# A three-stage transformer kernel on one NeuronCore: first-stage waits and row statistics moved, the first expert block's weights in halves

## The chip, the cores and the metric

The kernel runs on one core of a Trainium2 chip. A core has TensorE (matmuls, PE in the rows, its weight loads PEld), VectorE (DVE), ScalarE (ACT), GpSimd (POOL) and SyncE (SP), which here only issues transfers. Each engine runs its own queue in order, and engines wait for one another by semaphores: `wait_ge(s, n)` holds the queue until s has reached n. The metric is the device time of the whole program in microseconds (us), the median of several runs.

## The reference

Four layers follow one another on x of 8 x 512 tokens of 256 numbers, each added to x with a gate:

```python
x = x + tanh(g_xattn[0]) * L0_xattn(layernorm(x), ctx, ctx)   # attention among the 16 heads of one token
x = x + tanh(g_ffn[0])   * L0_ffn(layernorm(x))               # 256 -> 1024 -> 256, quantised to 8 bits
x = x + tanh(g_xattn[1]) * L1_xattn(ctx, layernorm(x), mask)  # masked cross attention, 512 x 512 per head
x = x + tanh(g_ffn[1])   * L1_ffn(layernorm(x))               # 8 experts, 2 for each token
# L0 attention: score = einsum('bsid,bsjd->bsij', Q, K) / 4, softmax over j, times V
# an expert: (silu(x @ w1) * (x @ w3)) @ w2, weighted by the token's share
```

## The kernel before

x lies in SBUF as `X`, 32 tiles of 128 tokens. Three functions run in turn, with a barrier between them.

`first_layer` computes the first two layers in rounds t = -3 to 38; in one round different tiles are at different steps. For tile t: statistics of its rows, `normalise`, transposes and three projections on TensorE (`qkv`), copies of them on ScalarE (`kv_copy`, `q_copy`), products of queries and keys split between VectorE (`own_scores`) and GpSimd (`scores`), the sum of the products on TensorE (`add_scores`), `largest` on VectorE, `exp` on ScalarE, products with the values on VectorE (`own_values`) and GpSimd (`weighted`, line 296), their sums on VectorE (`other_values`, line 602), and the output projection. The feed-forward part of a pair of tiles runs some rounds behind; its row statistics are taken by ScalarE (`f_statistics`, lines 426 to 432), and GpSimd turns them into deviations (`f_deviations`, lines 273 and 275). The order in each engine's queue is that of the calls in its loop over the rounds.

The statistics ahead of `normalise` are made differently: VectorE takes them for whole parts of X (`x_stats`, line 666: tiles 0 to 3, 4 to 15, 16 to 31) and GpSimd makes the deviations of a part at once (`x_deviations`, line 266). The parts are three loads (`x_part`). VectorE also splits the biases of the projections into three bfloat16 rows (`split_biases`), and ScalarE sends these to three partitions (`bias3`, line 418). TensorE starts its rounds when the four weights and `bias3` are in (`w_in` at 5 x 16). ScalarE copies the feed-forward weights at the end of round -1 (`f_weights`, lines 508 to 511), and VectorE makes `w1_lo` from it (line 647).

`cross_attention` is the second stage; of it only two counters of constants change. At its end tokens are scattered to their experts' rows in `expert_in`.

`experts` works through 39 blocks of 256 or 128 rows (`slot`), all of one expert each. Every weight is split in a high and a low part, and a product takes three matmuls. For block j: SP loads w1, w3, w2 of its expert into `raw` (one buffer for each of the three; `load_weights`, line 1758; the next block may load when the low part is made, `lo_done`), ScalarE makes the high part (`high_part`, line 1764), VectorE the low part (`low_part`, line 1768). TensorE computes `hidden`: for f = 0 to 7 the products with w1 and w3 (12 matmuls, line 1918), ScalarE silu (line 1989), VectorE the product `gated` (line 2033); part f of 4 and over waits for `gated` f - 3. Then TensorE transposes the next block's rows (`turn`, line 1911) and does `project` with w2 in four pairs of f, each after its low part (`g_parts`). In block j ScalarE makes the high parts of block j + 1 after silu 1, 3 and 5, and VectorE the low parts after gates 1 and 5 and after the gates. The first two blocks' expert is known early; the expert and first row of the others come from a chain of small one-partition operations of VectorE (lines 2068 to 2107, the last releases `blocks_known`), four of them wide (from line 2092, 592 elements). After that VectorE makes block 0's low parts. Ahead of block 0 TensorE waits for the first high part and runs 16 matmuls of the identity (line 1953).

## Time and profile before

| | us |
|---|---|
| median of 3 runs (2059.53 to 2062.3) | 2061.55 |
| the profiled execution's own time | 2063.94 |
| its span, first to last instruction | 2062.2 |
| busy: TensorE / VectorE / ScalarE / GpSimd | 1892.7 / 1552.3 / 1145.8 / 935.7 |
| first stage, second stage, experts (about) | 0 to 514, to 1375, to 2062 |

The numbers of an instruction come from one execution, so they are compared with its own time. A time in brackets behind an instruction is how long its engine sat idle ahead of it, and the arrow names what ended that.

### The profile page before, as it was taken

Reading aid. Unit: us, or ns where it says so; the run is one execution under the profiler, and the core shown is the slowest. Engines: PE = TensorE matmul, PEld = TensorE weight load, DVE = VectorE, ACT = ScalarE, POOL = GpSimd, SP = SyncE. Lnnn points to the kernel's source line nnn. Section 1 sums busy time; section 2 is a strip of 40 time slices with the busy share of each in tenths; the row PEclk is TensorE's granted clock in tenths of the full one; section 3 lists DMA queues with packets and bytes.
Section 4 is the critical chain, followed back from the end, with each engine's and each line's share of the span. In section 5 each row is a group of like instructions: output and inputs, shape, how many; then the busy total and the mean of one; then the engine's idle time right before and its main releaser. Section 6 shows DMA issues by size and latency. Waiting matters only on the chain. (4 is left out here: it accounts for less than half of the span.)

```text
span 2062.2 us, 35515 instructions
## 1 busy us (share of the span) xinstructions
PE 1892.7 (92%) x12100; PEld 1339.9 (65%) x12100; DVE 1552.3 (75%) x3251; ACT 1145.8 (56%) x2414; POOL 935.7 (45%) x674
## 2 busy tenths in 40 slices
PE   4899999986889999998999999959999999999998
PEld 2566776664543434443434343449999999999998
DVE  7999999992566677777767678657777777777785
ACT  2356666655336555555555555516665665656563
POOL 6999999981633334343534351023222231222322
PEclk9999999997999999999999999979999999999999
DMA  5222222210425051524242423037666666666662
GB/s 176 114 93 114 91 113 114 108 37 1 116 65 124 27 129 53 123 68 108 68 110 73 104 92 77 19 108 251 238 224 234 229 230 209 226 226 231 231 226 89
DMA packets 138569, 271.45 MB, mean 132 GB/s; under 512 B 13244, under 2 KB 90256, under 8 KB 132499
## 3 DMA queue, kind: packets, MB, share of 16 engines
q1 hardware_dynamic: 127916, 243.63, 37.9%
q0 software_dynamic: 9952, 25.25, 3.3%
q8 instruction: 99, 1.62, 0.3%
q14 instruction: 84, 0.68, 0.1%
q10 hardware_dynamic: 518, 0.27, 0.0%
HBM read 200.12 MB, written 70.47 MB: 131 GB/s over the span
## 5 line engine op out<-in xcount | busy, mean ns | idle before, releaser
L1476 DVE CUSTOM_DVE_ANT_0 x_dump<-x_ps,x_bias_q 128x512 bf16<-128x512 f32 x512 | 353.1, 690 | 103.0 <-PE x_ps L1160 90.1
L1345 ACT ACTIVATE x_PT<-x_ps 128x512 f32<-128x512 f32 x512 | 292.2, 601 | 230.6 <-PE x_ps L1175 227.4
L1989 ACT ACTIVATE X<-m_ps 128x256 f32<-128x256 f32 (+1 forms) x312 | 113.1, 363 | 222.0 <-PE m_ps L1918 219.6
L1160 PE MATMUL x_ps<-x_KS,x_QS 96*128 96x512 bf16 x512 | 198.1, 387 | 23.1 <-DVE x_mx L1476 22.2
L1872 POOL DMA_INDIRECT out_dram<-e_y,e_label x71 | 71.6, 1008 | 321.6 <-DVE e_y L2051 302.2
L1174 PE MATMUL x_ps<-x_bias_k,x_ident_b 128*128 128x512 bf16 x512 | 196.6, 384 | 2.8 <-DMA x_QS<-x_rows 1.7
L1175 PE MATMUL x_ps<-x_QS,x_KS 98*128 98x512 bf16 x512 | 196.5, 384 | 0.0
L1918 PE MATMUL m_ps<-e_x_lo,m_hi 128*128 128x256 f32 (+1 forms) x640 | 180.1, 281 | 4.5 <-issue 4.5
L1918 PE MATMUL m_ps<-e_x_hi,m_hi 128*128 128x256 f32 (+1 forms) x640 | 180.0, 281 | 0.0
L1918 PE MATMUL m_ps<-e_x_hi,m_lo 128*128 128x256 f32 (+1 forms) x640 | 179.9, 281 | 0.0
L2033 DVE TENSOR_TENSOR X<-X,m_ps 128x256 f32<-128x256 f32 (+1 forms) x312 | 114.0, 394 | 83.8 <-ACT X L1989 80.0
L1864 POOL DMA_INDIRECT e_y<-out_dram,e_label x71 | 101.8, 1434 | 164.8 <-DMA out_dram<-e_y,e_label 83.2
L296 POOL TENSOR_TENSOR a_pool_pv<-a_e,a_v 128x2304 f32<-128x2304 f32 x32 | 162.8, 5087 | 16.0 <-ACT a_e L478 16.0
L1918 PE MATMUL m_ps<-e_x_hi,e_hi 128*128 128x256 f32 (+1 forms) x608 | 169.8, 279 | 0.0
L1918 PE MATMUL m_ps<-e_x_hi,e_lo 128*128 128x256 f32 (+1 forms) x608 | 169.5, 279 | 0.0
L1918 PE MATMUL m_ps<-e_x_lo,e_hi 128*128 128x256 f32 (+1 forms) x608 | 169.5, 279 | 0.0
L1768 DVE TENSOR_TENSOR m_lo<-m_raw,m_hi 128x2048 fp32r<-128x2048 f32 x60 | 137.3, 2288 | 28.8 <-ACT m_hi L1764 28.8
L1768 DVE TENSOR_TENSOR e_lo<-m_raw,e_hi 128x2048 fp32r<-128x2048 f32 x57 | 130.4, 2287 | 26.8 <-ACT e_hi L1764 26.8
L1160 PEld LDWEIGHTS x_ps<-x_KS,x_QS 96*128 96x128 bf16 x512 | 50.1, 98 | 135.5 <-DVE x_mx L1476 104.9
L1918 PEld LDWEIGHTS m_ps<-e_x_lo,m_hi 128*128 128x128 f32 x640 | 121.8, 190 | 4.6 <-issue 4.6
L1918 PEld LDWEIGHTS m_ps<-e_x_hi,m_lo 128*128 128x128 f32 x640 | 121.8, 190 | 0.0
L1918 PEld LDWEIGHTS m_ps<-e_x_hi,m_hi 128*128 128x128 f32 x640 | 121.7, 190 | 0.0
(344 smaller groups left out, 5413.5 us busy)
## 6 DMA issues: line engine op xcount, KB each, us to landing
m_raw<-in_L_ffn_w_dram SPq DMA_DIRECT2D x117, 1024.0 KB, 5.1
expert_in<-a_blank SPq DMA_DIRECT2D x34, 1032.0 KB, 4.4
parts<-x_part SPq DMA_DIRECT2D x24, 512.0 KB, 3.8
m_x<-expert_in SPq DMA_DIRECT2D x32, 258.0 KB, 4.9
next_mask_k<-in_maskT_dram SPq DMA_DIRECT2D x32, 256.0 KB, 2.6
next_mask_q<-in_mask_dram SPq DMA_DIRECT2D x29, 256.0 KB, 2.8
x_KS<-parts SPq DMA_DIRECT2D x16, 384.0 KB, 11.3
x_QS<-parts SPq DMA_DIRECT2D x8, 576.0 KB, 6.7
```

Source lines behind the costliest of these rows:

```text
L296: pool.tensor_tensor(heads(pool_pv[:, :], PV_POOL), probabilities(e_[t % 2][:, PV_OWN * H:], PV_POOL), values(v_sb[t % 3][:, :], PV_POOL), ...
L1160: pe.matmul(ps_max[m % 2], QS[b % 2][0:HROWS, h, q * P:(q + 1) * P], KS[b % 2][0:HROWS, h, :], start=True, stop=True).then_inc(s1_ps, 1)
L1174: pe.matmul(ps_st[e % 3], ident_b[:, :], bias_k[b % 2][:, kc, :], start=True, stop=False)
L1175: pe.matmul(ps_st[e % 3], KS[b % 2][:, h, kc * P:(kc + 1) * P], QS[b % 2][0:HROWS + MROWS, h, :], start=False, stop=True).then_inc(st_read ...
L1345: act.activation(PT[unit % 2][:, k, :], ps_st[e % 3], ACT.Exp, scale=DH ** -0.5).then_inc(exp_done, 1)
L1476: dve.tensor_tensor_reduce(out=dump[:, :], in0=ps_max[m % 2], in1=bias_q[b % 2][:, q, :], scale=1.0, scalar=NEG, op0=ALU.add, op1=ALU.max, ...
L1768: eng.tensor_tensor(w_lo[p][n][:, :, :], raw[n][:, :, :], w_hi[p][n][:, :, :].bitcast(F32), ALU.subtract)\
L1864: pool.indirect_dma_start(out=yb[p][:, n, :], out_offset=None, in_=rows, in_offset=tokens(p, n), bounds_check=T - 1, oob_is_err=False).the ...
L1872: pool.indirect_dma_start(out=rows, out_offset=tokens(p, n), in_=yb[p][:, n, :], in_offset=None, bounds_check=T - 1, oob_is_err=False).the ...
L1918: mm = pe.matmul(out, left[a], right[b], start=first and n == 0, stop=last and n == 2)
L1989: act.activation(silu[f % 2][:, 0:wide], ps_h[f % 4][:, 0:wide], ACT.Silu).then_inc(silu_done, 1)
L2033: dve.tensor_tensor(gated[k % 2][:, n, 0:wide], silu[n][:, 0:wide], ps_h[f % 4][:, BLK:BLK + wide], ALU.mult)\
```

## The change

**First stage.** TensorE's wait for all five transfers goes; `qkv(0)` waits for the four weights ahead of its first product and for `bias3` (a semaphore of its own) ahead of the matmul that adds it. ScalarE issues the `bias3` transfer after `normalise(0)` in round -3 instead of ahead of everything. SP waits for its landing ahead of `x_part(1)` and all that it issues later. `x_stats(1)` and `x_stats(2)` on VectorE and their `x_deviations` on GpSimd go. In their place ScalarE takes the statistics of tile t + 6 at the end of round t (`row_statistics`, with the steps of `f_statistics`), and GpSimd makes the deviations of two tiles at the start of every even round (`row_deviations`). **Second stage.** Two table writes count on `consts` instead of on a semaphore of their own. **Experts.** Block 0's w1 and w3 are loaded in halves of the 1024 columns, first halves first; high and low parts follow in halves. VectorE does `x_low(0, 0)` and the low parts of the first halves ahead of the wide table operations, those of the second halves after the tables, and the low part of block 0's w2 in block 0, after gate 3. TensorE starts `hidden(0)` with the first halves and waits for the second ahead of f = 4. Block 1's loads wait for both halves (`EXTRA` = 1, 1, 0). 14 matmuls of the identity instead of 16 run without a wait. The diff, without declarations and the second stage's counters:

```diff
@@ -214,6 +215,7 @@
             context(1)
+            sp.wait_ge(bias3_landed, 16)
@@ -267,6 +269,14 @@
+            def row_deviations(b):
...
+                pair, n = slice(2 * b, 2 * b + 2), b - TPB // 2
+                pool.wait_ge(row_stats, 2 * n + 2)
+                pool.tensor_tensor(mu_rs[:, 1, pair], eps_t[:, pair], half[:, pair], ALU.pow).then_inc(rstd_done, 1)
+                pool.wait_ge(rstd_done, n + 2)
+                pool.tensor_tensor(shift[:, pair], shift[:, pair], mu_rs[:, 1, pair], ALU.mult).then_inc(shift_done, 1)
@@ -297,10 +307,9 @@
             x_deviations(0)
-            x_deviations(1)
...
-                if t == 0:
-                    x_deviations(2)
+                if t % 2 == 0 and TPB <= t + 4 < NT:
+                    row_deviations((t + 4) // 2)
@@ -319,10 +328,14 @@
                 pe.wait_ge(c_in[t % 2], 16 * (t // 2 + 1))
+                if t == 0:
+                    pe.wait_ge(w_in, 4 * 16)
...
+                if t == 0:
+                    pe.wait_ge(bias3_landed, 16)
@@ -386,7 +399,6 @@
             pe.wait_ge(consts, 5)
-            pe.wait_ge(w_in, 5 * 16)
@@ -414,14 +426,22 @@
             act.activation(tg[:, :], gl[:, :], ACT.Tanh).then_inc(tanh_done, 1)
-            act.wait_ge(bias_split, 1)
-            act.dma_start(bias3[:, :], bias_parts[:, :, :]).then_inc(w_in, 16)
...
+            def row_statistics(t):
...
+                act.wait_ge(x_in[[t in tiles for tiles in PARTS_OF_X].index(True)], 16)
+                act.wait_ge(f_means, 1)
+                statistics(t, row_stats)
...
+                statistics(t, f_stats)
...
+            def statistics(t, ready):
@@ -429,7 +449,7 @@
                 steps.wait()
-                act.activation(eps_t[:, t:t + 1], sums[:, t:t + 1], ACT.Identity, bias=epsilon[:, :], scale=1.0 / D).then_inc(f_stats, 1)
+                act.activation(eps_t[:, t:t + 1], sums[:, t:t + 1], ACT.Identity, bias=epsilon[:, :], scale=1.0 / D).then_inc(ready, 1)
@@ -444,7 +464,7 @@
-                wait(act, shift_done, 1 + [t in tiles for tiles in PARTS_OF_X].index(True))
+                act.wait_ge(shift_done, 1 if t < TPB else t // 2 - TPB // 2 + 2)
@@ -521,6 +541,9 @@
                     normalise(t + 3)
+                if t == -3:
+                    act.wait_ge(bias_split, 1)
+                    act.dma_start(bias3[:, :], bias_parts[:, :, :]).then_inc(bias3_landed, 16)
@@ -539,6 +562,8 @@
                     f_statistics(t - 1)
+                if TPB <= t + 6 < NT:
+                    row_statistics(t + 6)
@@ -623,7 +648,6 @@
             split_biases(4, bias_row, bias_rest, bias_parts)
-            x_stats(1)
@@ -640,8 +664,6 @@
                     own_scores(t + 2)
-                if t == -2:
-                    x_stats(2)
@@ -1015,9 +1037,9 @@
                 pool.memset(ones_b[:, :], 1.0).then_inc(consts, 1)
-                pool.iota(iota_i[:, :], pattern=[[1, NE]], base=0, channel_multiplier=0).then_inc(tables, 1)
-                pool.iota(token[:, :], pattern=[[P, NT]], base=0, channel_multiplier=1).then_inc(tables, 1)
-                pool.wait_ge(consts, 16)
+                pool.iota(iota_i[:, :], pattern=[[1, NE]], base=0, channel_multiplier=0).then_inc(consts, 1)
+                pool.iota(token[:, :], pattern=[[P, NT]], base=0, channel_multiplier=1).then_inc(consts, 1)
+                pool.wait_ge(consts, 18)
@@ -1752,9 +1777,15 @@
                               else expert[0:1, bass.ds(k, 1)], min_val=0, max_val=NE - 1)
+            if isinstance(j, int) and j == 0:
+                for h in HALVES_OF:
+                    for n, w in enumerate((w1, w3)):
+                        sp.dma_start(raw[n][:, :, h], w[e].rearrange("(c p) n -> p c n", p=P)[:, :, h])\
+                            .then_inc(w_raw_in[n] if h.start else half_in, 16)
+                sp.dma_start(raw[2][:, :, :], w2[e].rearrange("(c p) n -> p c n", p=P)).then_inc(w_raw_in[2], 16)
+                return
...
-                if not (isinstance(j, int) and j == 0):
-                    sp.wait_ge(lo_done[n], j)
+                sp.wait_ge(lo_done[n], j + EXTRA[n])
@@ -1764,9 +1795,24 @@
         def low_part(eng, j, p, n):
-            eng.wait_ge(hi_done[n], j + 1)
+            eng.wait_ge(hi_done[n], j + 1 + EXTRA[n])
...
+        def first_high(act):
...
+            for h in HALVES_OF:
+                for n in range(2):
+                    act.wait_ge(*((w_raw_in[n], 16) if h.start else (half_in, 32)))
+                    act.activation(w_hi[0][n][:, :, h], raw[n][:, :, h], ACT.Copy).then_inc(hi_done[n], 1)
+            high_part(act, 0, 0, 2)
...
+        def first_low(dve, h):
...
+            for n in range(2):
+                dve.wait_ge(hi_done[n], 2 if h.start else 1)
+                dve.tensor_tensor(w_lo[0][n][:, :, h], raw[n][:, :, h], w_hi[0][n][:, :, h].bitcast(F32), ALU.subtract)\
+                    .then_inc(lo_done[n], 1)
@@ -1885,8 +1931,8 @@
                 for p in range(2):
-                    pool.memset(yb[p][:, :, :], 0.0).then_inc(blanks, 1)
-                pool.wait_ge(blanks, 2)
+                    pool.memset(yb[p][:, :, :], 0.0).then_inc(iotas, 1)
+                pool.wait_ge(iotas, 7)
@@ -1920,10 +1966,14 @@
                     j, p, wide = at_slot(i, q), q % 2, tiles_in(q) * P
+                    first = isinstance(j, int) and j == 0
...
-                        pe.wait_ge(lo_done[n], j + 1)
+                        pe.wait_ge(lo_done[n], 1 if first else j + 2)
...
+                        if first and f == FC // 2:
+                            for n in range(2):
+                                pe.wait_ge(lo_done[n], 2)
@@ -1948,8 +1998,7 @@
                 turn(0, 0)
-                pe.wait_ge(hi_done[0], 1)
-                for _ in range(16):
+                for _ in range(14):
@@ -1994,8 +2043,7 @@
                 x_high(0, 0)
-                for n in range(3):
-                    high_part(act, 0, 0, n)
+                first_high(act)
@@ -2036,6 +2084,8 @@
                             low_part(dve, j + 1, 1 - p, k // 2)
+                        if isinstance(j, int) and j == 0 and k == 1:
+                            low_part(dve, 0, 0, 2)
@@ -2089,6 +2139,8 @@
                 wide = lambda a: a[:, :, :].unsqueeze(2).broadcast_to([1, 2, LISTED, NE])
+                x_low(0, 0)
+                first_low(dve, HALVES_OF[0])
@@ -2105,9 +2157,7 @@
                 dve.tensor_scalar(expert[:, :], n_past[:, 0, :], float(NE - 1), None, ALU.min).then_inc(blocks_known, 1)
-                x_low(0, 0)
-                for n in range(3):
-                    low_part(dve, 0, 0, n)
+                first_low(dve, HALVES_OF[1])
```

## Rows read from the trace of the kernel before

**Rows 1.** Two stretches: busy PE, PEld, DVE, ACT, POOL; clock, DMA, GB/s.

```profile
60.00:450.00 390.00, 362.25 (x1885) 264.05 (x1884) 372.34 (x353) 233.80 (x702) 373.07 (x144) 0.98 0.25 100
...
1396.00:1740.00 344.00, 339.52 (x2897) 339.35 (x2896) 262.92 (x380) 206.31 (x324) 88.06 (x77) 1.00 0.68 232
```

**Rows 2.** Timeline, start: start us, us, engine, line, operation, output<-input, count, [idle before].

```profile
10.68 1.30 ACTq L418 DMA_DIRECT2D a_bias<-a_bias_parts  x1
...
15.09 4.02 DVE L666 BATCH_NORM_STATS2 stats<-X 128x6 f32<-128x256 f32 x12 [4.44 <-DMA X<-in_x_dram]
...
16.23 0.66 PE L315 MATMUL a_ps<-ident_f,a_xn 128*128 128x128 f32 x2 [16.23 <-DMA a_bias<-a_bias_parts]
...
26.79 5.32 DVE L666 BATCH_NORM_STATS2 stats<-X 128x6 f32<-128x256 f32 x16 [0.86 <-DMA X<-in_x_dram]
...
28.13 1.90 ACT L508 ACTIVATE a_w_hi<-a_w 128x2048 fp32r<-128x2048 f32 x1
```

**Rows 3.** DMA issues: tiles, queue, count, KB each, us from issue to landing.

```profile
X<-in_x_dram SPq DMA_DIRECT2D x1, 512.0 KB, 3.9
...
next_bias<-a_next_parts SPq DMA_DIRECT2D x3, 1.5 KB, 1.7
```

**Rows 4.** Timeline, first rounds, VectorE and GpSimd.

```profile
37.40 4.39 DVE L647 TENSOR_TENSOR a_w_lo<-a_w,a_w_hi 128x2048 fp32r<-128x2048 f32 x1
...
46.47 5.04 POOL L296 TENSOR_TENSOR a_pool_pv<-a_e,a_v 128x2304 f32<-128x2304 f32 x1
...
51.55 2.56 DVE L602 TENSOR_REDUCE a_ps<-a_pool_pv 128x144 f32<-128x2304 f32 x1 [0.19 <-POOL a_pool_pv L296]
...
59.04 5.05 POOL L296 TENSOR_TENSOR a_pool_pv<-a_e,a_v 128x2304 f32<-128x2304 f32 x1
```

**Rows 5.** Timeline, two late rounds of the first stage.

```profile
424.15 5.08 POOL L296 TENSOR_TENSOR a_pool_pv<-a_e,a_v 128x2304 f32<-128x2304 f32 x1 [1.21 <-ACT a_e L478]
...
430.59 0.42 ACT L426 ACTIVATE a_spare<-X 128x256 f32<-128x256 f32 x1
...
432.00 0.29 ACT L432 ACTIVATE a_eps<-a_sums,a_epsilon 128x1 f32<-128x1 f32 x1
...
434.26 0.71 POOL L273 TENSOR_TENSOR mu_rs<-a_eps,a_half 128x2 f32<-128x2 f32 x1
...
435.20 2.37 POOL L291 TENSOR_TENSOR a_pool_qk<-a_pool_qk 128x1024 f32<-128x1024 f32 x1
...
435.93 0.44 PE L315 MATMUL a_ps<-ident_f,a_on 128*128 128x128 f32 x2 [0.49 <-DVE a_on L606]
```

**Rows 6.** Timeline, ahead of the expert blocks and at block 1.

```profile
1380.54 0.76 DVE L2092 TENSOR_TENSOR X<-X 1x592 f32<-1x592 f32 x1
...
1386.29 0.17 DVE L2107 TENSOR_SCALAR m_expert<-X 1x37 int32<-1x37 f32 x1
...
1386.65 1.91 ACT L1764 ACTIVATE m_hi<-m_raw 128x2048 fp32r<-128x2048 f32 x1 [5.82 <-DMA m_raw<-in_L_ffn_w_dram]
...
1388.60 2.29 DVE L1768 TENSOR_TENSOR m_lo<-m_raw,m_hi 128x2048 fp32r<-128x2048 f32 x1 [1.46 <-ACT m_hi L1764]
...
1389.27 1.91 ACT L1764 ACTIVATE m_hi<-m_raw 128x2048 fp32r<-128x2048 f32 x1 [0.70 <-DMA m_raw<-in_L_ffn_w_dram]
...
1412.90 0.28 PE L1918 MATMUL m_ps<-e_x_lo,e_hi 128*128 128x256 f32 x1
```

**Rows 7.** Timeline of SP's queue: issue of block 1's three weight loads.

```profile
1391.06 5.56 SPq L1758 DMA_DIRECT2D m_raw<-in_L_ffn_w_dram  x3
```

**Rows 8.** Weight loads of later blocks (line 1758), from issue to landing.

```profile
DMA to landing us min/median/max: 4.8/5.0/7.0
```

**Rows 9.** Timeline, the same four matmuls of TensorE after work and after idleness.

```profile
27.32 1.13 PE L350 MATMUL a_ps<-a_pool_qk,ident_f 128*128 128x256 f32 x4
...
42.73 2.04 PE L350 MATMUL a_ps<-a_pool_qk,ident_f 128*128 128x256 f32 x4 [3.80 <-DVE a_sm L586]
```

**Rows 10.** The page's costliest groups: busy us, mean ns, idle before, releaser.

```profile
L2033 DVE TENSOR_TENSOR X<-X,m_ps 128x256 f32<-128x256 f32 (+1 forms) x312 | 114.0, 394 | 83.8 <-ACT X L1989 80.0
```

More of the change, by code:

```diff
@@ L164, in first_layer @@
         act_chain, f_means = sem("act_chain"), sem("f_means")
+        bias3_landed, row_stats = sem("bias3_landed"), sem("row_stats")
         slices = lambda a, n: a.rearrange("p (d i j) -> p d i j", d=n, i=H)
@@ L886, in cross_attention @@
         m_ready, m_free, inverted = sem("m_ready"), sem("m_free"), sem("inverted")
-        gate_in, x_out, tables = sem("gate_in"), sem("x_out"), sem("tables")
+        gate_in, x_out = sem("gate_in"), sem("x_out")
         g_stats, g_rstd, g_xn, g_xT, gap, e2_done = (sem(n) for n in ("g_stats", "g_rstd", "g_xn", "g_xT", "gap", "e2_done"))
@@ L909, in wait @@
                 eng.wait_ge(semaphore, count)
-        CONSTS = 20
+        CONSTS = 22
         block = ctx.enter_context(nc.Block())
@@ L1526, in gate_tables @@
             def gate_tables():
-                dve.wait_ge(tables, 2)
+                dve.wait_ge(consts, CONSTS)
                 do(dve.tensor_copy(iota_e[:, :], iota_i[:, :]))
@@ L1737, in experts @@
         hi_done, lo_done = [sem(f"hi_done{n}") for n in range(3)], [sem(f"lo_done{n}") for n in range(3)]
+        half_in = sem("half_in")
+        EXTRA = (1, 1, 0)
+        HALVES_OF = (slice(0, FF // 2), slice(FF // 2, FF))
         h_ps, y_ps = sem("h_ps"), sem("y_ps")
@@ L1822, in experts @@
             g_high, y_left, y_out = sem_("g_high"), sem_("y_left"), sem_("y_out")
-            labelled, blanks, before_in = sem_("labelled"), sem_("blanks"), sem_("before_in")
+            labelled, before_in = sem_("labelled"), sem_("before_in")
             passed = sem_("passed")
```

## Prediction

> **What bounds the kernel now.** I read four views in this order. The table by stretches tells which engine sets the pace: in the first stage VectorE and GpSimd are both busy over 95% of 390 us, ScalarE 60% [rows 1]; in the expert blocks TensorE is busy 98.7% (2897 matmuls in 339.5 us, 0.117 us each) [rows 1]. So a microsecond taken out ahead of either stretch comes off the end, and work added to ScalarE alone is free as long as it delays nobody. The timeline of the first 60 us tells what the first round waits for: TensorE starts at 16.23, released by the landing of `bias3`, which was issued at 10.68 [rows 2]. The rounds after that are gapless on VectorE and GpSimd: `other_values(0)` waits 0.19 us for GpSimd's product, the only such wait [rows 4]. The timeline between routing and experts shows VectorE's table operations hidden behind the first weight load, then three high/low pairs in a row [rows 6].
>
> **First stage, start.** Removed: the wait for `bias3` ahead of everything, and VectorE's statistics of tiles 4 to 31. The wait moves behind the first transposes and k/v matmuls. Bound for the landing of `bias3`: its issue ends at 10.68 + 1.30 = 12.0 [rows 2]; a similar transfer between buffers takes 1.7 us from its issue of about 0.6 [rows 3], so 13.1, against 16.2 now; bounds 12.4 and 14.5. The k/v matmuls for tile 0 run before that, and the first queries come some 6 us sooner.
> The cost of it: SP now issues the second part of X, both feed-forward weights and the third part only at 13.1. The first part, 512 KB, lands 3.9 us after its issue [rows 3]; tiles 4 to 31 and the weights run at 4096 KB in 26.79 - 15.09 = 11.7 us, 350 KB/us [rows 2]. So the second part lands at 13.1 + 3.9 + 1024/350 = 19.9, 20.5 with its longer issue (1536 KB instead of 512), the weights 5.9 later, at 26.4, and the third part and the context tile behind it at about 32.5. Now they land at 15.1, some 21 and 26.8. Hence the new late thing: `f_weights` (two copies of 1.90 and a short one, 4.0 us [rows 2]) ends at 30.4 instead of 32.1, and `row_statistics(5)` queues behind it on ScalarE. Its four steps cost what `f_statistics` costs, 430.59 to 432.29 = 1.7 us [rows 5]: 32.1. GpSimd waits for this in `row_deviations(2)`, with `scores(1)` and `weighted(0)` queued behind: 0.94 us (434.26 to 435.20 [rows 5]) gives 33.1, the scores cost 59.04 - 51.51 = 7.5 [rows 4], so `weighted(0)` starts at 40.7 instead of 46.47 [rows 4]: **5.8 us sooner**. VectorE comes out alike, since `exp(0)` sits behind the copies of tile 2, whose context tile lands at 32.5.
> Inside that sum is one gain that hangs on timing. `w1_lo` (4.39) now lies beside GpSimd's product [rows 4]; a VectorE operation of the same size takes 2.29 in the experts [rows 6]. In the new order it falls at 28 to 31, while GpSimd waits. If it slid beside `scores(1)` it would cost 2 us. The Trainium skill (SBUF — State Buffer, "SBUF: two separate sides") says that such an operation with two SBUF inputs and a GpSimd operation that reads SBUF exclude each other for the whole instruction. By that rule, the trace agrees (4.39 against 2.29), and a slip would make the sum 2 us worse.
>
> **First stage, rounds.** Added per round: 1.7 us of ScalarE at its end (28 rounds), and per two rounds 0.94 us of GpSimd (13 more pairs, the first is counted above); the two wide power operations, which were off the rounds' path or at its start, go. GpSimd's cover in every even round is its wait of 1.21 us for `e` [rows 5]; 0.27 is left. ScalarE's next transposed copy comes some 1.7 later and pushes the query matmul by about 0.35 in even rounds; the cover is TensorE's idle 0.49 ahead of the output transposes [rows 5]. Both fit. In the first six rounds GpSimd's margin is smaller and I count 0.3 lost. If one of the covers is gone, 13 pairs x 0.3 = 4 us. Nothing is queued behind the new `half`, `f_means` waits that isn't long ready. **Stage: -5.5, bounds -7.0 and -3.8.**
>
> **Second stage.** `consts` absorbs `tables`: the waits that count to 22 are met far ahead. Zero. The same for `blanks`.
>
> **Experts.** Each of the way-in weights comes as two halves. Now w1 and w3 are ready for ScalarE at 1386.65 and 1389.25, 2.6 apart, the high part takes 1.91, the low part 2.29 [rows 6]. Halves: w1's first at about 1385.3, w3's first at 1386.65, high part of it (half of 1.91) 1387.65, low part (half of 2.29) 1388.85. TensorE could start there instead of about 1395.5 (1412.90 [rows 6] less block 0's 144 matmuls of 0.117 us and its transposes). But the table operations from L2092 on, 1380.54 to 1386.46 = 5.92 us [rows 6], are now queued **behind** these low parts. Today they lie wholly under the load; this cover is given up, and VectorE idles in its stead from about 1381.7 to 1386.3. They end at 1394.8, the low parts of the second halves at 1395.95 and 1397.1.
> TensorE has four of eight hidden parts by then and waits. That alone would be good: part four at 1397.6 against 1401. What is late next is block 1. `raw` has one buffer; SP may load block 1's w1 only when both low halves are done, at 1395.95, where now it is issued at 1391.06 [rows 7]. A load takes 5.0 us to land (4.8 to 7.0) [rows 8]. ScalarE has block 1's high part in its queue behind the second silu, VectorE its low part behind the second gate. Step by step: landing 1401.0, high part 1403.0, low part 1405.3; only then gates 2 and 3, which TensorE's part six waits for. Two gates (0.39 each [rows 10]) and a remainder of about 0.6: 1406.6. Then comes the moved low part of block 0's w2, 2.29: 1408.9. SP waits for exactly this one to load block 1's w2: landing 1413.9, high part 1415.9, and ScalarE's silu 6 and 7, with gates 6 and 7 and the last remainders, are behind it. Five short steps of 0.4 to 0.6: 1418.3. Then TensorE has two of four pairs of block 0's projection left, 24 matmuls, 2.8 us: block 1 starts at 1421.1 instead of 1412.90 [rows 6]. That is +8.2. TensorE has idled twice by then, over 5 and over 3 us. After an idle 3.80 us four matmuls took 2.04 [rows 9], where the same four took 1.13 after work [rows 9]: the 1.2 GHz level. So the 24 and perhaps some more run at nearly double time, +1.5 to +3.3. I take +1.8. **Experts: +10, bounds +7 and +12.** The 14 warm-up matmuls instead of 16, now free from 1380.2, are off the path.
> For the two loads the Trainium skill (DMA: Bandwidth & Descriptors, "Two cost components") gives a fixed 2.0 us and bytes/436e9 seconds, 4.4 us for 1 MB. Here rows show 5.0. By the page the experts would cost 1.2 us less.
>
> **The sum.** -5.5 + 10 = +4.5. The profiled execution took 2063.94 us, its span 2062.2; it would become 2068.4. It lies 2.4 above the median of the runs, 2061.55, and so I forecast **2066.0**.
>
> **Rivals.** (a) The clock stays at 2.4 GHz through the waits, or the landings take 4.8: experts +7 to +8.2, stage -6: +1.7, **2063.2**. For it: the second idle, 3.3 us, is shorter than the 3.80 after which the level was low [rows 9]. Against it: the first one is longer, and little work lies between. (b) **Faster:** block 1's loads don't stop block 0. The price is one mechanism: TensorE's second half then starts at 1397.6 instead of 1401, -3.4, and with -5.5 it is -8.9, **2052.7**. It decides at the landing of block 1's w2: it would have to be there by about 1401, and the order of the low parts puts its issue at 1408.9. Only an order of the queues other than I read lets it happen. (c) **Slower still:** the rounds lose their covers (GpSimd 0.27, TensorE 0.14 per pair are small), +4: **2070**. For it: both engines at 95%. Against it: each pair has its own wait to give. (d) The first stage gains nothing because the late transfers hold ScalarE: in (c)'s place too, since it gives +4 to +5.
>
> **Chances.** The forecast (2064 to 2069) 0.50, (a) 0.25, (b) 0.13, (c) and (d) 0.12. A measurement can tell 0.2%, 4.1 us: slower begins at 2065.7, in the middle of the likeliest case, whose own range is 2063.5 to 2069. Slower: half of the forecast and more, and (c), (d): 0.42. Same: the rest of the forecast, (a): 0.44. Faster: 0.14. The range leaves out (b) and the far end of (c): 2057 to 2070.
>
> **What would show it.** TensorE's first transpose at 9 to 10 and its bias matmul at about 13; `weighted(0)` at 40 to 42; the second weights copied from 26 on; rounds of 27.3 us per pair unchanged, with GpSimd's wait for `e` down to 0.3. In the experts: table operations ending at 1394.8 less the first stage's gain, TensorE waiting some 5 us after the sixth part and again ahead of the third projection pair, ScalarE waiting for `m_raw` twice about 5 us. Wrong would be: `bias3` landing later than 14.5; block 1 starting less than 7 us behind its old place; rounds longer than 27.4 per pair.

## The result and the profile after

The changed kernel takes 2089.97 us (median of 4 runs, 2089.49 to 2092.56), the kernel before 2061.93 in the runs beside it (2059.53 to 2063.67). The ratio is 1.0142, 95% interval 1.0126 to 1.0158: slower by 28 us, where 2066.0 with 2057 to 2070 was forecast. The profiled execution has a span of 2090.7 us against 2062.2.

Two marks split the span into the three stages: GpSimd's first `x_ones` write begins the second stage, its first IOTA of the experts begins the third. First two lines of before, then the same two of after (start, duration, engine, line, operation):

```profile
514.41 0.19 POOL L1004 MEMSET x_ones<- 3x128 bf16 x1 [29.24 <-POOLq L90]
1374.78 0.15 POOL L1875 IOTA X<- 1x30 int32 x1 [13.27 <-POOLq L803]
```

```profile
535.06 0.20 POOL L1026 MEMSET x_ones<- 3x128 bf16 x1 [29.22 <-POOLq L90]
1390.66 0.15 POOL L1921 IOTA X<- 1x30 int32 x1 [14.55 <-POOLq L825]
```

The first stage lost 20.65 us, the second took 855.6 instead of 860.4, and the experts took 700.0 instead of 687.4. So -5.5 became +20.65, 0 became -4.8, and +10 became +12.6.

**The start came as forecast, a little better.** Timeline of after, SP, ScalarE, TensorE and GpSimd:

```profile
9.70 0.66 PE L324 MATMUL a_ps<-ident_f,a_xn 128*128 128x128 f32 x2 [9.70 <-ACT a_xn L469]
12.79 0.37 SPq L202 DMA_DIRECT2D X<-in_x_dram  x1
19.74 0.42 ACT L446 ACTIVATE a_spare<-X 128x256 f32<-128x256 f32 x1 [3.21 <-DMA X<-in_x_dram]
25.66 1.91 ACT L528 ACTIVATE a_w_hi<-a_w 128x2048 fp32r<-128x2048 f32 x1 [1.70 <-DMA a_b<-in_b_dram]
31.94 3.78 PE L335 MATMUL a_ps<-a_wkv,a_cT 128*128 128x512 f32 x4 [4.96 <-DMA a_cT<-in_ctxT_dram]
39.86 5.08 POOL L306 TENSOR_TENSOR a_pool_pv<-a_e,a_v 128x2304 f32<-128x2304 f32 x1
```

TensorE begins at 9.70 instead of 16.23 [rows 2]; `weighted(0)` starts at 39.86 instead of 46.47 [rows 4], 6.6 us sooner. From there to the end of the stage it is 495.2 us instead of 467.9: the rounds lost 27.3.

**The rounds lost it at one wait.** The table of waits of GpSimd between 60 and 460 us (engine, line waited for, releaser: us in total, times, longest), first before, then after:

```profile
POOL a_pool_pv L296 <- ACT a_e L478: 15.1, 13, 1.4
```

```profile
POOL mu_rs L276 <- ACT a_eps L452: 27.8, 12, 3.3
```

The old wait for `e`, the 1.21 of [rows 5], is gone, and a new one stands in `row_deviations`. Timeline of after, one even round, GpSimd and the last step of `row_statistics` on ScalarE:

```profile
402.60 5.06 POOL L306 TENSOR_TENSOR a_pool_pv<-a_e,a_v 128x2304 f32<-128x2304 f32 x1
...
409.00 0.29 ACT L452 ACTIVATE a_eps<-a_sums,a_epsilon 128x1 f32<-128x1 f32 x1
...
409.37 0.71 POOL L276 TENSOR_TENSOR mu_rs<-a_eps,a_half 128x2 f32<-128x2 f32 x1 [1.70 <-ACT a_eps L452]
410.16 0.20 POOL L278 TENSOR_TENSOR a_shift<-a_shift,mu_rs 128x2 f32<-128x2 f32 x1
410.31 2.81 POOL L292 TENSOR_TENSOR a_pool_qk<-a_q,a_k 128x1536 f32<-128x1536 f32 x1
...
417.91 5.07 POOL L306 TENSOR_TENSOR a_pool_pv<-a_e,a_v 128x2304 f32<-128x2304 f32 x1
...
431.27 5.08 POOL L306 TENSOR_TENSOR a_pool_pv<-a_e,a_v 128x2304 f32<-128x2304 f32 x1
```

GpSimd is free at 407.66 and waits for statistics that end at 409.29, the last thing ScalarE does in its round. All of `scores` and `weighted` stands behind that wait. From 402.60 to 417.91 it is 15.3 us; an even round of before took 13.9, its wait for `e` included. The pair of rounds, to 431.27, takes 28.7 us; a pair of before took 27.3. VectorE pays with it: its busy time in 390 us of rounds fell from 372 to 352, GpSimd's from 373 to 358 (by stretches, same columns as [rows 1], where the clock is TensorE's granted one), ScalarE's rose to 259:

```profile
60.00:450.00 390.00, 355.14 (x1801) 257.85 (x1799) 351.68 (x333) 259.18 (x814) 358.23 (x159) 0.96 0.26 100
```

**The experts lost by the mechanism that was forecast.** Timeline of after around block 0, ScalarE, VectorE, SP and TensorE:

```profile
1402.82 2.36 DVE L1814 TENSOR_TENSOR m_lo<-m_raw,m_hi 128x1024 fp32r<-128x1024 f32 x2 [4.12 <-ACT m_hi L1807]
1405.28 0.36 PE L1964 MATMUL m_ps<-e_x_lo,m_hi 128*128 128x256 f32 x1 [3.83 <-issue]
1411.94 2.34 DVE L1814 TENSOR_TENSOR m_lo<-m_raw,m_hi 128x1024 fp32r<-128x1024 f32 x2
1413.31 12.98 SPq L1789 DMA_DIRECT2D m_raw<-in_L_ffn_w_dram  x3
1418.20 1.91 ACT L1795 ACTIVATE e_hi<-m_raw 128x2048 fp32r<-128x2048 f32 x1 [7.15 <-DMA m_raw<-in_L_ffn_w_dram]
1422.82 0.58 PE L1964 MATMUL m_ps<-e_x_lo,m_hi 128*128 128x256 f32 x1 [4.98 <-DVE X L2081]
1423.61 2.28 DVE L1799 TENSOR_TENSOR m_lo<-m_raw,m_hi 128x2048 fp32r<-128x2048 f32 x1
1433.09 1.91 ACT L1795 ACTIVATE e_hi<-m_raw 128x2048 fp32r<-128x2048 f32 x1 [9.05 <-DMA m_raw<-in_L_ffn_w_dram]
1437.17 0.58 PE L1964 MATMUL m_ps<-m_lo,e_g_hi 128*128 128x256 f32 x1 [6.20 <-DVE e_g_lo L2093]
```

Read it from the start of the stage, 1390.66, as all of the experts below. Block 0 begins after 14.6 us (20.4 before), but block 1's first load is issued after 22.7 (16.3 before [rows 7]), its w2 only when the low part of 1423.61 has ended, and block 1 starts after 50.9 instead of 38.1. TensorE stands still twice, 4.98 and 6.20 us, and its granted clock is 0.50 in the 3.2 us behind the first of these waits (1422.8 to 1426.0).

### The profile page after: what moved, and what is told of

Its sections match the earlier page's. It is cut to its first block and busy times, and to the rows that moved or that the text cites. A ratio compares the mean times of both kernels' runs of the same rounds, so it can differ in the third digit from the quotient of the medians.

```text
span 2090.7 us, 35685 instructions
## 1 busy us (share of the span) xinstructions
PE 1905.5 (91%) x12096; PEld 1349.5 (65%) x12096; DVE 1539.8 (74%) x3193; ACT 1188.3 (57%) x2584; POOL 932.3 (45%) x698
## 3 DMA queue, kind: packets, MB, share of 16 engines
q1 hardware_dynamic: 128460, 243.63, 37.3%
## 5 line engine op out<-in xcount | busy, mean ns | idle before, releaser
L1910 POOL DMA_INDIRECT e_y<-out_dram,e_label x71 | 97.2, 1369 | 164.6 <-DMA out_dram<-e_y,e_label 82.9
L1799 DVE TENSOR_TENSOR m_lo<-m_raw,m_hi 128x2048 fp32r<-128x2048 f32 x58 | 132.7, 2288 | 26.6 <-ACT m_hi L1795 26.6
L1964 PEld LDWEIGHTS m_ps<-e_x_lo,m_hi 128*128 128x128 f32 x640 | 123.2, 193 | 15.9 <-issue 10.7
## 6 DMA issues: line engine op xcount, KB each, us to landing
x_KS<-parts SPq DMA_DIRECT2D x16, 384.0 KB, 10.9
```

Source lines behind the costliest of these rows:

```text
L1799: eng.tensor_tensor(w_lo[p][n][:, :, :], raw[n][:, :, :], w_hi[p][n][:, :, :].bitcast(F32), ALU.subtract)\
L1910: pool.indirect_dma_start(out=yb[p][:, n, :], out_offset=None, in_=rows, in_offset=tokens(p, n), bounds_check=T - 1, oob_is_err=False).the ...
L1964: mm = pe.matmul(out, left[a], right[b], start=first and n == 0, stop=last and n == 2)
```

## The experiments

**Theory 1**: the first stage's loss is GpSimd's wait for row statistics that ScalarE makes at the end of its round; the experts' loss is two delays that add, the table operations ahead of block 1's w1 and w3, and the moved low part of w2 ahead of its w2; the stages don't touch each other. The rivals stand in each expectation. The readings of all runs, with the two marks from each profile ("stage 1" is the first mark, "stage 2" the distance between the two, "block 1" its first matmul behind the second mark, "weighted(0)" its start; ratio to the kernel before on the same chip). The marks come from one execution of each kernel, and the same code moves them: the first stage of before ended at 514.4 to 517.7 in its five profiles, and with the experts of before block 1 came after 36.1 to 38.1 in six, so smaller differences than these in a column say nothing by themselves:

| kernel | weighted(0) | stage 1 | stage 2 | block 1 | ratio (95% interval) |
|---|---|---|---|---|---|
| before | 46.5 | 514.4 | 860.4 | 38.1 | |
| after | 39.9 | 535.1 | 855.6 | 50.9 | 1.0142 (1.0126 to 1.0158) |
| first stage's part | 39.9 | 533.1 | 863.7 | 36.4 | 1.0107 (1.0072 to 1.0142) |
| - row_deviations moved | 37.9 | 509.4 | 857.7 | 36.4 | 0.9964 (0.9949 to 0.9980) |
| - statistics a round earlier | 42.8 | 511.9 | 854.5 | 36.1 | 0.9983 (0.9968 to 0.9999) |
| - moved, SP free | 37.5 | 506.3 | 855.3 | 37.3 | 0.9948 (0.9931 to 0.9965) |
| waits at use alone | 47.1 | 516.9 | 859.5 | 37.2 | 1.0001 (0.9989 to 1.0014) |
| experts' part | 46.8 | 515.7 | 859.8 | 49.7 | 1.0066 (1.0049 to 1.0083) |
| - tables first | 46.8 | 514.5 | 857.2 | 44.7 | 1.0039 (1.0019 to 1.0059) |
| - w2 low early | 46.8 | 514.7 | 858.8 | 41.3 | 1.0022 (1.0005 to 1.0040) |
| - both | 47.0 | 517.7 | 856.9 | 36.3 | 0.9995 (0.9980 to 1.0010) |
| both stages mended | 36.4 | 507.5 | 856.5 | 35.2 | 0.9956 (0.9941 to 0.9972) |
| - 34 warm-up matmuls | 39.2 | 508.8 | 858.8 | 36.2 | 0.9969 (0.9950 to 0.9987) |
| - 14 again, SP free | 36.3 | 502.9 | 858.9 | 35.5 | 0.9960 (0.9946 to 0.9975) |

### The first stage's part alone

The experts and the counters of the second stage are those of before.

> The first stage's part of the change alone; the experts are those of before. Theory 1 (the loss lies in the rounds and comes from GpSimd's wait for late row statistics, 35.6 us in 14 waits in the trace of after; the experts lose 12.8 more on their own account): second stage begins at 535, as in after, against 514.4 before; experts begin at 1390.6; time 2061.9 + 15.9 = 2078. Rival A (the two stages' losses depend on each other, for instance the second stage's 4.75 us gain is a late gift of the first stage's order): second stage begins at 535, but the time is 2082, the full 20.65 later. Rival B (most of the loss is the experts'): time under 2070.

2083.6 us, ratio 1.0107, slower than the 2078 of theory 1. The waits in `row_deviations` are the same 27.8 us in 12, the second stage begins at 533.1. The loss is the first stage's; rival B is out. Rival A's 2082 fits the time better, but not its reason: the second stage, here word for word that of before, took 863.7, 3.3 more than in the profile of before, while theory 1 had counted with 4.75 less. Both lie among the 854.5 to 863.7 of the unchanged second stages in the table.

### row_deviations behind the preceding scores

```diff
-                if t % 2 == 0 and TPB <= t + 4 < NT:
-                    row_deviations((t + 4) // 2)
...
                 if block is not None:
                     f_deviations(block)
+                if t % 2 == 1 and TPB <= t + 3 < NT:
+                    row_deviations((t + 3) // 2)
                 pool.wait_ge(a_made, t + 1)
```

> The first stage's part with one thing moved: GpSimd's row_deviations stands behind the products of the preceding scores instead of ahead of them, one step later on GpSimd; same work on each engine. Theory 1 (the wait is the loss): GpSimd's 35.6 us of waits for the row statistics fall under 5, rounds return to 27.3 us per pair, the start's gain of 6.6 stays, second stage begins at 508 to 510, time 2055 to 2057. Rival C (the added work itself is the loss: 1.7 us of ScalarE in 28 rounds and 0.94 of GpSimd in 14, each pair of rounds 1.7 longer whatever the order): time stays at 2074 to 2079. Between them: the wait is a part only, and another engine becomes late next, 2060 to 2070.

2054.3 us, ratio 0.9964: the same operations on the same engines, one of them later in its queue, and 29 us are back. GpSimd's waits between 60 and 460 us:

```profile
POOL a_pool_pv L308 <- ACT a_e L498: 7.5, 15, 1.2
POOL mu_rs L283 <- ACT a_eps L452: 4.6, 1, 4.6
```

No wait in `row_deviations` (L276) is left, and the wait for `e` has fallen from 15.1 to 7.5: part of the 12.2 us of `row_deviations` (13 x 0.94) lies in it now. The 4.6 is a single wait in `f_deviations` (L283). From `weighted(0)` to the end of the stage it is 471.5 us, against 467.9 before and 495.2 in after. The timeline of this kernel shows what the change had asked for. In an even round GpSimd is free at 409.46, and the statistics end at 413.01, 3.55 later:

```profile
409.46 2.82 POOL L292 TENSOR_TENSOR a_pool_qk<-a_q,a_k 128x1536 f32<-128x1536 f32 x1
...
412.72 0.29 ACT L452 ACTIVATE a_eps<-a_sums,a_epsilon 128x1 f32<-128x1 f32 x1
...
418.34 5.08 POOL L308 TENSOR_TENSOR a_pool_pv<-a_e,a_v 128x2304 f32<-128x2304 f32 x1 [1.24 <-ACT a_e L498]
```

Rival C, the added work itself, is out: 1.7 us of ScalarE a round and 0.94 of GpSimd a pair of rounds cost 3.6 us in this trace, not 27.

### The statistics one round earlier

```diff
-                if TPB <= t + 6 < NT:
-                    row_statistics(t + 6)
+                if TPB <= t + 7 < NT:
+                    row_statistics(t + 7)
```

> The first stage's part with ScalarE making each tile's row statistics one round earlier; GpSimd's row_deviations stands where the change has it, ahead of the scores. It takes the wait away from the other side than the run with the move. Theory 1 (the loss is GpSimd waiting for a result that ScalarE makes at the end of its round): no waits of the longest 3.3 us in the rounds, second stage begins within 2 us of the run with the move, 508 to 511, time 2053 to 2057 where after's first stage alone gave 2083.6. Rival F (the place of row_deviations on GpSimd is itself the loss, since 0.94 us ahead of scores makes them late for TensorE): second stage still 10 us or more behind, time over 2070.

2057.0 us, ratio 0.9983; the second stage begins at 511.9, 0.9 later than the theory allowed. GpSimd's waits between 60 and 460 us:

```profile
POOL mu_rs L283 <- ACT a_eps L452: 5.5, 1, 5.5
POOL a_pool_pv L306 <- ACT a_e L498: 3.3, 3, 1.4
```

The wait is gone from this side too, with `row_deviations` (L276) where the change has it: rival F is out. The distance to the run above, 2.4 us at the first mark, lies ahead of the rounds: `weighted(0)` is 4.9 later, and from there to the end of the stage it is 469.1 us against 471.5. The first `row_statistics` now stands in ScalarE's first round and waits there for the second part of X, with the copies of the first queries behind it, which come at 24.19 instead of 16.02 in the first stage's part alone:

```profile
24.19 0.32 ACT L488 ACTIVATE a_q<-a_ps 128x176 f32<-128x176 f32 x1 [1.94 <-PE a_ps L345]
```

### The waits at their use alone

Of the first stage only TensorE's waits and the place of the `bias3` issue are changed; `x_stats`, `x_deviations` and SP's queue stay.

> Of the first stage's part only the waits at their use: TensorE waits for bias3 and the weights where it uses them, ScalarE issues bias3 in its first round, the statistics stay on VectorE and GpSimd, and SP isn't held for bias3. It asks what the start's 6.6 us are made of. Theory (the first stage begins as soon as the inputs allow, but exp(0) and own_pv wait on VectorE, which still has x_stats(1) and x_stats(2) ahead of the rounds): weighted(0) at 43 to 46.5 instead of 46.47, time 0 to 3 us under before, 2058 to 2061. Rival (the waits alone are the whole gain, and row statistics on ScalarE give nothing): weighted(0) at 40, time 2054 to 2056.

Ratio 1.0001, `weighted(0)` at 47.1: no gain, though TensorE starts at 9.59. `bias3` lands 1.72 us behind TensorE's need of it, and the two statistics stand in VectorE's queue among the first tiles' products, where they wait for X:

```profile
15.76 4.02 DVE L681 BATCH_NORM_STATS2 stats<-X 128x6 f32<-128x256 f32 x12 [5.11 <-DMA X<-in_x_dram]
27.43 5.32 DVE L681 BATCH_NORM_STATS2 stats<-X 128x6 f32<-128x256 f32 x16 [2.56 <-DMA X<-in_x_dram]
...
43.56 2.02 DVE L605 TENSOR_TENSOR a_own_pv<-a_ps,a_v 128x1792 f32<-128x1792 f32 x1 [0.33 <-ACT a_ps L489]
```

The first `own_pv` starts at 43.56; it was 42.92 before and 38.71 in after. So the waits alone are worth nothing here. The next run has them too and leaves SP's queue alone like this one, but takes the row statistics off VectorE, and there `weighted(0)` starts at 37.5: the start's gain needs that. The statistics moved alone, with the old waits, weren't run.

### SP not held for bias3

```diff
             context(1)
-            sp.wait_ge(bias3_landed, 16)
             x_part(1)
```

> The first stage's part with row_deviations moved, and without SP's wait for bias3 ahead of the second part of X. It asks which part the held SP queue plays in the start. Theory (the wait keeps the small bias3 from sharing the queues with 1.5 MB of X and 2 MB of weights, but everything large then lands some 3 us later and ScalarE's f_weights and the third context tile with it): without it bias3 lands at 15 to 16 instead of 12.8, the first queries come 2 to 3 us later, the weights land 2 to 3 us sooner, weighted(0) at 36 to 40, within 2 us of 37.9; time 2053 to 2057. Rival (bias3 is all that counts): weighted(0) at 41, time 2057 to 2060.

2051.2 us, ratio 0.9948. `bias3` lands at 16.1 instead of 12.8, and TensorE waits for it at the addition:

```profile
16.13 0.60 PE L338 MATMUL a_ps<-a_bias,a_ones 3*128 3x512 bf16 x1 [1.80 <-DMA a_bias<-a_bias_parts]
```

Yet `weighted(0)` starts at 37.5, as with the wait (37.9): SP issues the weights from 6.58 instead of 13.14 and the third part of X at 14.80 instead of 18.97, and the third tile's queries are copied at 34.36 instead of 37.00 (each against the run with the move and the wait). The rival is out. The first stage is 3.1 us shorter than with the wait, but the intervals of the two ratios overlap, and unchanged first stages differ by as much.

### The experts' part alone

> The experts' part alone; first and second stage are those of before. Theory 1 (table operations moved behind the first halves' low parts, and block 0's w2 low part moved into the block, delay block 1's weights, whatever comes before): experts begin at 1374.7 as before, block 1's first matmul at 1412.9 + 12.8 = 1425.7, time 2061.9 + 12.8 = 2074.7. Rival (the delay in after came from something that the first stage's part changed, such as the clock or the tables' place): block 1 at 1413 to 1421, time 2062 to 2070.

2075.4 us, block 1 after 49.7. The delay is there without the first stage's part; its rival is out. Seen from the median it costs 14.7, by the ratio 13.6. The ratios of the two parts, 1.0107 and 1.0066, add up to 1.0173 against 1.0142 for the whole change; their intervals cover the difference.

### Tables first

```diff
-                x_low(0, 0)
-                first_low(dve, HALVES_OF[0])
...
                 dve.tensor_scalar(expert[:, :], n_past[:, 0, :], float(NE - 1), None, ALU.min).then_inc(blocks_known, 1)
+                x_low(0, 0)
+                first_low(dve, HALVES_OF[0])
                 first_low(dve, HALVES_OF[1])
```

> The experts' part, but with the table operations ahead of x_low and the first halves' low parts, as before; block 0's w2 low part still stands inside block 0. Theory 1 in two parts: the tables' delay holds block 1's w1 and w3 loads (about 5 us of the 12.8), the moved w2 low part holds block 1's w2 load (the rest). Then this kernel has block 1's w1 and w3 loads issued at about 1391 but w2's only after VectorE has passed block 0's second gate: time 2061.9 + 3 to + 7 = 2065 to 2069. Rival D (the tables alone are the loss): time 2060 to 2062. Rival E (the w2 low part alone is the loss, the tables cost nothing by themselves): time 2073 to 2075.

Block 1 after 44.7, 2067.2 us. Its loads of w1 and w3 are issued 16.3 us into the stage, as before, but w2's waits for the moved low part (one line stands for three issues with waits between them, so 14.38 us):

```profile
1387.93 14.38 SPq L1767 DMA_DIRECT2D m_raw<-in_L_ffn_w_dram  x3
1411.44 0.58 PE L1942 MATMUL m_ps<-m_lo,e_g_hi 128*128 128x256 f32 x1 [6.20 <-DVE e_g_lo L2071]
```

### w2's low part early

```diff
-                        if isinstance(j, int) and j == 0 and k == 1:
-                            low_part(dve, 0, 0, 2)
...
                 first_low(dve, HALVES_OF[1])
+                low_part(dve, 0, 0, 2)
```

> The experts' part with block 0's w2 low part right behind the second halves' low parts, ahead of block 0's gates; the table operations stay where the change has them. Block 1's first matmul counted from GpSimd's first IOTA at the experts' start: 38.1 before, 50.9 in after, some 44.6 with the tables first (that trace). Theory 1 (two delays that add: tables some 7 us on w1 and w3, the w2 low part on w2): here w2's load is issued right behind w3's, only the tables' delay is left, 41 to 44. Rival E (the w2 low part alone is the loss): 38 or less. Rival D (the tables alone are): 50. Time 2060.8 + 3 to + 6.

Block 1 after 41.3, within the 41 to 44 of theory 1.

### Both taken back in the experts

> The experts' part with both taken back: table operations ahead of the low parts, w2's low part ahead of block 0's gates. What is left of the change is the halves alone. Theory 1: block 0's first matmul 5.5 us sooner than before (15.1 from the first IOTA, as with the tables first), block 1's weights issued no later than before, block 1's first matmul at 34 to 36 instead of 38.1; time 2 to 4 us under before, 2057 to 2059. Rival (the halves themselves cost: more and shorter transfers, four copies instead of two, block 1's loads sharing the queues): block 1 at 38 to 42, time 2061 to 2065.

Block 1 after 36.3, ratio 0.9995. The four runs make a square: with neither delay 36.3, with the tables' 41.3 (+5.0), with w2's 44.7 (+8.4), with both 49.7 (+13.4). The two delays add, as closely as one profile of each can tell, which settles theory 1 against rivals D and E. But what is left, the halves alone, gave no time where 2 to 4 us were expected: 36.3 lies among the 36.1 to 38.1 of the experts of before. Block 0 begins 5.2 us sooner than before, and at the lower clock. TensorE had idled 5.65 us behind its warm-up, and the first 27 matmuls go at the 1.2 GHz level (most 0.41 us each, 0.21 apart; granted clock 0.50 from 1389.8 to 1395.5) before they return to 2.4 (0.28, 0.12 apart; 1.00 from 1395.7 to 1400):

```profile
1389.80 0.55 PE L1942 MATMUL m_ps<-e_x_lo,m_hi 128*128 128x256 f32 x1 [5.65 <-DVE m_lo L1792]
...
1395.27 0.41 PE L1942 MATMUL m_ps<-e_x_hi,m_lo 128*128 128x256 f32 x1
...
1395.68 0.28 PE L1942 MATMUL m_ps<-e_x_lo,m_hi 128*128 128x256 f32 x1
```

### Both stages mended

The whole change of the first stage and the experts, with `row_deviations` moved, the tables first and w2's low part early; the second stage's counters are those of before.

> The whole change with both stages mended: row_deviations behind the preceding scores' products, table operations ahead of the low parts, w2's low part ahead of block 0's gates. Theory 1 (the stages' parts are independent): first stage 5 us under before, as in the run with that move alone (509.4 against 514.4), experts 2 to 4 under: 2051 to 2055. Rival (the gain of one stage is lost in the other): 2056 to 2061.

2054.2 us, ratio 0.9956. First stage -6.9, block 1 after 35.2: neither part loses in the presence of the other. It isn't faster than the first stage's part with `row_deviations` moved (0.9964, the intervals overlap).

### 34 warm-up matmuls

> The version with both stages mended, with 34 warm-up matmuls instead of 14. There TensorE idles 4.87 us between warm-up and block 0 and starts block 0 at the slow level (0.41 us a matmul for the first 14, 27 in the run with the experts' part mended alone, 0.28 after). Theory 1 (this slow start, 0.1 us a matmul, and two short waits for VectorE eat most of what the halves gain: block 1 starts 35.2 after the first IOTA against 36.4 without the experts' part): idle gone, no slow matmuls, block 1 at 33.5 to 34.5. Rival (block 1's start is set by its weights' landing and low parts, not by TensorE): 35 to 36, time unchanged at 2054.

The idle time and the slow matmuls are gone (granted clock 1.00 from 1382.3 to 1390.0):

```profile
1373.36 8.96 PE L2002 MATMUL m_ps<-ident_f 128*128 128x128 f32 x68
1382.31 0.36 PE L1964 MATMUL m_ps<-e_x_lo,m_hi 128*128 128x256 f32 x1
1382.51 0.28 PE L1964 MATMUL m_ps<-e_x_hi,m_lo 128*128 128x256 f32 x1
```

Block 1 starts after 36.2, not sooner, and the ratio is 0.9969. The traces say what sets that start: ScalarE's first high part of block 1's weights. In the run with 14 warm-up matmuls, then in this one:

```profile
1384.79 1.92 ACT L1795 ACTIVATE e_hi<-m_raw 128x2048 fp32r<-128x2048 f32 x1 [0.79 <-DMA m_raw<-in_L_ffn_w_dram]
```

```profile
1389.70 1.92 ACT L1795 ACTIVATE e_hi<-m_raw 128x2048 fp32r<-128x2048 f32 x1 [2.04 <-DMA m_raw<-in_L_ffn_w_dram]
```

Both are released by the landing of w1, 20.8 and 22.1 us into the stage, and block 1 starts 14.4 and 14.1 us behind them. This distance is 13.7 to 14.4 us in all ten profiles of kernels with neither of the two delays, whether block 0 began at the lower clock or not, and with the tables' delay alone it is 13.7 as well (27.6 to 41.3). The load is issued 15.9 us into the stage in both runs (16.3 before); here it took 6.2 us to land, there 4.9. So the rival holds: the slow start isn't what ate the halves' gain, and a sooner block 0 only waits longer, as its later parts need gates that stand behind block 1's high and low parts in the queues of ScalarE and VectorE. No run loads block 1's weights sooner.

### Both stages mended, SP not held

> The version with both stages mended (row_deviations moved, tables first, w2's low part early, 14 warm-up matmuls), without SP's wait for bias3. Parts so far, each against its own run of before: row_deviations moved 0.9964, the same without SP's wait 0.9948, both stages mended 0.9956, experts mended alone 0.9995. Theory (SP's wait is worth nothing or costs up to 3 us, the halves are worth 0 to 1 us): ratio 0.994 to 0.996, weighted(0) at 36 to 38. Rival (the two add: the wait costs 3 us in every run, and the halves give 2): 0.992 to 0.9935.

2053.2 us, ratio 0.9960: the theory's range, and the rival is out. The first stage is 4.6 us shorter than with SP's wait (502.9 against 507.5), as it was 3.1 in the other pair; the whole times don't show it (0.9960 against 0.9956), and unchanged first stages differ by 3.3, so what the wait is worth stays open. The five kernels with the move lie at 0.9948 to 0.9969, all faster than both given ones, and can't be told apart.

## Why the prediction was wrong, point by point

- **The start** was right, in its steps and not only in its end. `bias3` landed at 12.8 (forecast 13.1), the second part of X at 19.7 (20.5), the weights at 25.7 (26.4), the context tile at 31.9 (32.5), `weighted(0)` at 39.9 (40.7). `w1_lo` took 2.29 us in its new place, as assumed.
- **The step that failed** is this one: "GpSimd's cover in every even round is its wait of 1.21 us for `e` [rows 5]; 0.27 is left ... Both fit." It compares how long the new operation takes with the idle time that it falls into, and never asks when its input is ready at the place where it was put. The statistics in [rows 5] are of an odd round, with ScalarE's statistics ended at 432.29, ahead of 434.26. The even round of the same trace would have told: GpSimd is free at 415.33, and ScalarE's statistics end at 418.85:

```profile
415.33 2.79 POOL L282 TENSOR_TENSOR a_pool_qk<-a_q,a_k 128x1536 f32<-128x1536 f32 x1
...
418.55 0.30 ACT L432 ACTIVATE a_eps<-a_sums,a_epsilon 128x1 f32<-128x1 f32 x1
```

  `row_statistics` goes behind these, to 420.5, and `row_deviations` was put at 415.3: 5.2 us too early. What came is less (waits of up to 3.3, 2.3 in the mean), probably because ScalarE catches up in the longer rounds; no run shows that apart. The account of 60 to 460 us: waits 27.8 - 15.1 = 12.7, and 12 pairs of 0.9 us of work that no idle time covers any more, 10.9; together 23.6 of the 27.3 lost. The rest lies ahead of 60 us and at the end and isn't resolved. The prediction's own sign of being wrong, rounds longer than 27.4 us per pair, is what came: 28.7.
- The prediction had priced this work at 4 us if its covers went (rival c). That was the wrong unit: a queue that waits loses the wait and the cover, and all that stands behind it is late. Had the order been read, the forecast for the stage would stand as the three runs with the move and with SP's wait show it: -5.0 to -6.9, where -5.5 (bounds -7.0 and -3.8) was forecast, give or take the 3.3 us by which unchanged first stages differ.
- **The second stage**: forecast 0, measured -4.8. Its length was 854.5 to 863.7 us in the twelve experiments, all with the second stage of before. So this is the spread from one execution to another and says nothing of the change. What makes the spread stays open. It is also why a sum made against one execution can't be better than half of that spread, 4.6 us.
- **The experts**: mechanism right, in each step, size +12.6 by the length of the stage and +12.8 by block 1's start, instead of +10 (bounds +7 and +12). Counted from the stage's first IOTA: low parts of the second halves done at 23.6 (forecast 22.3), block 1's w1 landed at 27.5 (26.2), w2's low part done at 35.2 (34.1), w2 landed at 42.4 (39.1), block 1 at 50.9 (46.3, 48.1 with the slow clock). The mis-sized term is the landing of w2: 7.2 us behind the low part that releases its issue (1425.9 to 1433.1) instead of 5.0, just past the 4.8 to 7.0 of [rows 8]. The tables came 1.3 late. Part of this is chance: with the experts' part alone the same load took 5.4, and block 1 came after 49.7. The start that it was counted from, 38.1, is also the latest of the six profiles with the experts of before, so the true loss is rather more than 12.8 than less; the ratio of the experts' part gives 13.6. That TensorE would return at 1.2 GHz was right too: 0.58 and 0.41 us a matmul behind the idle times of 4.98 and 6.20.
- **The rivals**: (a), (b) and (d) were out; (c) had the place and a seventh of the size.

## What to carry to other kernels

When work moves from one engine's queue to another's, compare two times for each consumer: when its queue reaches it and when its input is ready, in every phase of a periodic schedule, even and odd. Durations against idle time only tell whether the work fits, not whether it waits. An operation with a late input belongs behind work whose inputs are there; moving it by one step in the queue was worth 29 us here. And an earlier start of a block was worth nothing here, where the next block's weights were loaded no sooner.

## What the runs showed of the hardware

- VectorE's `w1_lo` and GpSimd's products of queries and keys exclude each other, and the timeline of the kernel with both stages mended shows it to within 0.2 us. `w1_lo` starts at 27.50, when GpSimd's product has 1.19 us to go, and takes 3.34 instead of 2.29:

```profile
26.32 2.37 POOL L294 TENSOR_TENSOR a_pool_qk<-a_q,a_k 128x1280 f32<-128x1280 f32 x1
...
27.50 3.34 DVE L669 TENSOR_TENSOR a_w_lo<-a_w,a_w_hi 128x2048 fp32r<-128x2048 f32 x1
```

  It waits out the other's instruction, then runs at its own pace (1.05 more against 1.19 left). In eleven other traces the product has 0.36 to 2.25 us to go, and `w1_lo` takes longer by that remainder less 0.13 to 0.15 each time. It works the other way too. In the kernel before, the 4.39 us of `w1_lo` [rows 4] end at 41.79; GpSimd's next product starts in them and takes 4.41 instead of 2.36:

```profile
39.60 4.41 POOL L284 TENSOR_TENSOR a_pool_qk<-a_q,a_k 128x1280 f32<-128x1280 f32 x1
```

  In the profile this waiting is part of the busy time and not idle time. The Trainium skill (SBUF — State Buffer, "SBUF: two separate sides") says that a VectorE operation with two SBUF inputs and a GpSimd operation that reads SBUF shut each other out for the whole instruction, the one that starts first going ahead; the traces agree.
- A load of 1 MB took 7.2 us to land, where the load of w1 ahead of it took 4.9 (1413.3 to 1418.2), the same load 5.4 in the runs of the experts' part and with the tables first, and 5.0 is the median [rows 8]. Why is open. The Trainium skill (DMA: Bandwidth & Descriptors, "Two cost components") gives 2.0 us and bytes/436e9 seconds, an estimate of 4.4 us for 1 MB; neither of these two loads was that fast, and the measurement decides.
- Identical code of the second stage took 854.5 to 863.7 us in twelve profiles (857.2 to 863.7 in the four of one chip), a wider spread than most changes here are worth.
